# Adding the relative bias of windowed attention on VectorE instead of TensorE, and running the exponentials in place

## The chip, the cores and the metric

The kernel runs on one core of a Trainium2 chip. The metric is the device time of one execution in microseconds; three executions of the kernel before took 389.59, 389.60 and 390.54 us, median 389.6 us. The engines named below are those of the profile: PE (TensorE, matmuls; PEld is its weight load), DVE (VectorE), ACT (ScalarE), POOL (GpSimd) and SP (SyncE, which here only issues DMAs). Each engine works through its own instruction list in order, and the engines meet through semaphores.

## The reference

The input is `x`, 8 images of 64 channels and 32x32 pixels, float32. The first half is a window-attention block, the second a gated convolution block. What the change touches is the softmax of the attention:

```python
attn = jnp.einsum('bnhd,bmhd->bhnm', q * scale, k)          # 8x8 windows: N = 64 positions, 8 heads, d = 8
bias = rel_bias_table[REL_IDX.reshape(-1)].reshape(N, N, HEADS)
attn = attn + bias.transpose(2, 0, 1)[None]                  # the same bias for every window and image
attn = jax.nn.softmax(attn, axis=-1)
out = jnp.einsum('bhnm,bmhd->bnhd', attn, v).reshape(Bn, N, C)
return out @ w_proj + b_proj
```

Around it stand a layer norm before (over channels), the residual add, a second layer norm, an MLP with GELU, and then the second block: a pointwise convolution with ReLU, a gate that picks 32 of 64 channels per image, and three depthwise convolutions (3x3, 5x5, 7x7) fused with a pointwise one, computed on PE as one 7x7 convolution.

## The kernel before

Both halves of the batch lie side by side on the 128 partitions (two images of 64 channels), so 4 image pairs of 1024 pixels give 4096 columns, cut into `NG = 8` groups of `G = 512` columns. A group holds 8 windows of 64 pixels (times two images). The attention is a software pipeline written out by hand: each engine has a function `step(g, ...)`, and in the step of group g it also does the maxima pass of group g+1 (`nxt`), the first layer norm with keys and queries of group g+2 (`far`), and the projection, residual and second layer norm of group g-1 (`prev`). There are 8 steps. The order of the calls in `step` is the order on the engine; nothing else sets it.

What one step does for its own group g:

- PE, `scores(g, w)` for each window w = 0..7 writes a PSUM bank of 128x512 (128 rows = 64 keys of two images, 512 columns = 8 heads x 64 queries) by five passes of 512 columns: three of keys times queries in split precision (L793), one that adds the relative bias (L795, `reverse` times `rel`), one that subtracts each row's maximum (L796). Two banks, `PROB0` and `PROB0 + 1`, are used in turn: scores(g, w) waits until window w-2 has been read out.
- ACT, `exponentials(g, w)` (L558): exp from that bank to `probs` in SBUF, 128x512.
- PE, `weighted_values` (L809) and `sums` (L818) for windows 0 to 3 after the fourth exponential, and for windows 4 to 7 at the end of the step, both into the bank `PV`.
- DVE, `divide_by_sums(g, quad)`: a reciprocal (L1120) and a product (L1122), once for each half. The second half's one comes last in DVE's step and so runs beside the start of PE's next step.

The maxima pass of the next group: `scores_for_max(g+1, w)` on PE is two passes (L774, and L775 with the same `rel`, flipped), `take_maximum` on DVE is a reduction of one bank (L1106), with three banks in rotation; after the eighth, PE transposes the maxima (L779), DVE negates and spreads them (L1112 to L1115), and PE's next step begins with them.

Beside them on ACT, between the exponentials: four copies of the values (L553), two squares of the centred input (L512, L513), the evacuation of the projection (L562), the logarithm and exponential of the inverse deviation (L518, L520), the cast of the residual (L566), two more squares (L570, L571), and the evacuations of keys and queries with two casts (L528, L535, L543). On DVE: two casts and two subtractions that split the second layer norm's output (L1144 and L277), the residual add in two instructions (L1128), the products of the two layer norms (L1092, L1133), the low parts of keys and queries (L1096, L1101). On POOL: the low parts of the inputs of PE's mean and variance passes (L277 with `parts`).

After the last `scores`, POOL clears `images` with eight memsets (L438) for the second block.

## Time and profile before

| | |
|---|---|
| median of 3 runs | 389.6 us |
| the profiled execution: its time, its span | 388.71 us, 386.9 us |
| PE busy | 331.2 us (86% of the span) |
| DVE busy | 259.4 us (67%) |
| ACT busy | 182.3 us (47%) |
| POOL busy | 126.8 us (33%) |
| the attention steps, start of step 0 to end of step 7 | about 35.9 to 211.4 us |

The span is what the profiler covers; 1.8 us of the execution lie outside it. Busy time of an engine is the union of its instructions. A matmul of 512 columns lasts 0.39 us in its own record, but the next one starts 0.23 us after it; the chain of waits shows the 0.23. In the same way an instruction of DVE or ACT may start a little before the one ahead of it has ended.

### The profile page before, as it was taken

Reading aid. Unit: us, or ns where it says so; the run is one execution under the profiler, and the core shown is the slowest. Engines: PE = TensorE matmul, PEld = TensorE weight load, DVE = VectorE, ACT = ScalarE, POOL = GpSimd, SP = SyncE. Lnnn points to the kernel's source line nnn. Section 1 sums busy time; section 2 is a strip of 40 time slices with the busy share of each in tenths; the row PEclk is TensorE's granted clock in tenths of the full one; section 3 lists DMA queues with packets and bytes.
Section 4 is the critical chain, followed back from the end, with each engine's and each line's share of the span. In section 5 each row is a group of like instructions: output and inputs, shape, how many; then the busy total and the mean of one; then the engine's idle time right before and its main releaser. Section 6 shows DMA issues by size and latency. Waiting matters only on the chain.

```text
span 386.9 us, 6319 instructions
## 1 busy us (share of the span) xinstructions
PE 331.2 (86%) x2432; PEld 227.4 (59%) x2432; DVE 259.4 (67%) x342; ACT 182.3 (47%) x303; POOL 126.8 (33%) x80
## 2 busy tenths in 40 slices
PE   1767999999999999999999579991674997899994
PEld 1454667767677776767676234440353775677773
DVE  7566183684847758485774954479895992999921
ACT  5345538475674756666436579892330200111200
POOL 5451102212131221210206602229675418765000
PEclk9989999999999999999999969997595998999999
DMA  7522641122122122222110000930000857277731
GB/s 180 107 68 71 142 87 53 48 68 71 49 69 51 49 59 60 70 52 64 49 41 2 0 2 1 200 83 0 2 0 0 169 121 144 58 155 159 150 81 27
DMA packets 31147, 27.68 MB, mean 72 GB/s; under 512 B 21008, under 2 KB 27664, under 8 KB 31120
## 3 DMA queue, kind: packets, MB, share of 16 engines
q1 hardware_dynamic: 30544, 26.50, 30.2%
q10 hardware_dynamic: 576, 0.81, 0.9%
q8 instruction: 18, 0.29, 0.3%
q14 instruction: 9, 0.07, 0.1%
HBM read 3.82 MB, written 2.10 MB: 15 GB/s over the span
## 4 chain that ended last, share of the span: by engine, by line
PE 62%; DVE 23%; ACT 4%; issue 4%; POOL 4%; SPq 1%; DMA 0%; DVEq 0%; ACTq 0%; POOLq 0%
PE psum L1023 12%; PE psum L793 11%; PE psum L725 4%; PE psum L809 4%; PE psum L774 4%; PE psum L796 3%; PE psum L795 3%; PE psum L775 3%; PE psum L818 3%; DVE maxima L1106 3%; DVE whole_w L1315 3%; PE psum L938 2%; POOL conv_w L462 2%; PE psum L949 2%; PE psum L752 2%
## 5 line engine op out<-in xcount | busy, mean ns | idle before, releaser
L1023 PE MATMUL psum<-shifted,conv_w 128*128 128x512 f32 x336 | 91.4, 436 | 7.2 <-DVE conv_w L277 2.9
L1023 PEld LDWEIGHTS psum<-shifted,conv_w 128*128 128x128 f32 x336 | 67.4, 203 | 31.0 <-DVE conv_w L277 4.5
L558 ACT ACTIVATE probs<-psum 128x512 f32<-128x512 f32 x64 | 38.3, 599 | 50.2 <-PE psum L796 49.4
L793 PE MATMUL psum<-q_heads,k_blocks 128*128 128x512 f32 x192 | 59.1, 416 | 0.0
L1106 DVE TENSOR_REDUCE maxima<-psum 128x8 f32<-128x512 f32 x64 | 41.0, 684 | 23.8 <-PE psum L775 23.8
L277 POOL TENSOR_TENSOR parts<-x,parts 128x256 fp32r<-128x256 f32 (+1 forms) x21 | 18.8, 911 | 103.9 <-ACT parts L507 59.0
L793 PEld LDWEIGHTS psum<-q_heads,k_blocks 128*128 128x128 f32 x192 | 34.8, 188 | 13.6 <-issue 7.1
L681 ACT CAST conv_w<-whole_w 128x1792 fp32r<-128x1792 f32 x7 | 11.8, 1688 | 64.6 <-DVE whole_w L1319 64.6
L725 PE MATMUL psum<-parts,center_average 128*128 128x512 f32 x64 | 23.2, 446 | 17.7 <-DVE parts L277 16.5
L277 POOL TENSOR_TENSOR parts<-square_logvar,parts 128x512 fp32r<-128x512 f32 x14 | 18.1, 1290 | 53.5 <-ACT square_logvar L571 27.5
L455 POOL TENSOR_TENSOR whole_w<-small,weights 128x1792 f32<-128x1792 f32 x8 | 30.4, 3798 | 8.3 <-DVE conv_w L1329 4.7
L774 PE MATMUL psum<-k_heads,q_blocks 128*128 128x512 f32 x64 | 27.1, 423 | 4.8 <-DMA k_heads<-k_parts 3.4
L1120 DVE RECIPROCAL inv_sum<-psum 128x256 f32<-128x256 f32 x16 | 28.0, 1748 | 3.3 <-PE psum L818 3.2
L1315 DVE TENSOR_TENSOR whole_w<-whole_w,product 128x1280 f32<-128x1280 f32 x8 | 21.6, 2699 | 7.6 <-POOL whole_w L455 7.0
L775 PE MATMUL psum<-rel,reverse 128*128 128x512 f32 x64 | 25.9, 404 | 0.0
L725 PEld LDWEIGHTS psum<-parts,center_average 128*128 128x128 f32 x64 | 12.1, 207 | 23.2 <-DVE parts L277 9.8
L796 PE MATMUL psum<-minus_max,pick 128*128 128x512 f32 x64 | 25.2, 393 | 0.0
L795 PE MATMUL psum<-rel,reverse 128*128 128x512 f32 x64 | 25.1, 392 | 0.0
L446 POOL TENSOR_TENSOR images<-square_logvar,images 128x512 f32 (+1 forms) x8 | 12.5, 1568 | 31.6 <-ACT images L658 31.6
L1339 DVE SCALAR_TENSOR_TENSOR x<-psum,weights,x 64x512 f32<-64x512 f32 x16 | 12.0, 750 | 12.7 <-PE psum L1023 12.4
L938 PE MATMUL psum<-normed,mlp_w 128*128 128x512 f32 (+1 forms) x64 | 19.8, 452 | 0.0
L809 PEld LDWEIGHTS psum<-probs,v_blocks 128*32 128x32 f32 x1024 | 15.0, 110 | 8.0 <-issue 8.0
(138 smaller groups left out, 561.3 us busy)
## 6 DMA issues: line engine op xcount, KB each, us to landing
shifted<-images SPq DMA_DIRECT2D x32, 332.5 KB, 5.5
k_blocks<-k_parts SPq DMA_DIRECT2D x32, 128.0 KB, 2.8
q_heads<-q_parts SPq DMA_DIRECT2D x128, 32.0 KB, 2.0
k_heads<-k_parts SPq DMA_DIRECT2D x64, 32.0 KB, 1.9
out<-x SPq DMA_DIRECT2D x8, 256.0 KB, 3.0
x<-in_x SPq DMA_DIRECT2D x6, 256.0 KB, 5.8
x<-in_x SPq DMA_DIRECT2D x4, 128.0 KB, 4.3
weights<-in_weights ACTq DMA_DIRECT2D x1, 464.0 KB, 6.9
```

Of the source, the lines that this page charges most:

```text
L277: return engine.tensor_tensor(low, whole, high.bitcast(F32), ALU.subtract)
L558: act.activation(probs[:, w, :], psum[:, PROB0 + w % 2, :], ACT.Exp).then_inc(S["ac_probs"], 1)
L725: ins = pe.matmul(psum[:, bank, :], center_average[:, which, :], parts[:, part, :], start=part == 0, stop=part == 1)
L774: pe.matmul(max_bank(w), q_blocks[:, w, :], k_heads[:, :, w * T:(w + 1) * T], start=True, stop=False)
L775: pe.matmul(max_bank(w), reverse[:], rel[:, 0, :], start=False, stop=True).then_inc(S["pe_max"], 1)
L793: pe.matmul(bank, k_blocks[:, w // (NW // 2), k_part, w % (NW // 2), :], q_heads[:, q_part, :, w * T:(w + 1) * T], start=k_part + q_part = ...
L795: pe.matmul(bank, reverse[:], rel[:, 1, :], start=False, stop=False)
L796: pe.matmul(bank, pick[:, w, :], minus_max[:, :, :], start=False, stop=True).then_inc(S["pe_scores"], 1)
L809: pe.matmul(psum[32 * j:32 * j + 32, PV, p * T:(p + 1) * T], v_blocks[:, par, at:at + 32], probs[:, w, head * T:(head + 1) * T], start=hh ...
L1023: ins = pe.matmul(psum[:, CONV0 + bh, :], conv_w[bh][:, w_part, t, :], img[:, y:y + H - 1:2, x0:x0 + W], start=t == 0 and w_part + part == ...
L1106: dve.tensor_reduce(maxima[:, w * NH:(w + 1) * NH], max_bank(w).rearrange("p (h t) -> p h t", t=T), AX.X, ALU.max).then_inc(S["dv_max"], 1)
L1315: dve.tensor_tensor(window, window, product5[:], ALU.add).then_inc(S["dv_product"], 1)
```

## The change

The bias is added by DVE when it moves the scores out of PSUM, and the PE pass for it goes. For that the bias must lie in SBUF in the layout of the scores: PE makes it once, in the set-up, in the bank `PROB0`, and ACT copies it to the new tile `rel_by_key` (128x512). From then on DVE's `add_bias(g, w)` writes `probs` = scores + `rel_by_key`, and ACT's exponential reads and writes `probs` in place. PE's wait for a free bank is now a wait for DVE (`dv_biased`) where it was one for ACT (`ac_probs`). DVE's step gets eight more instructions, placed among the others by hand. The maxima pass keeps its own bias pass (L775).

```diff
             def exponentials(g, w):
-                act.wait_ge(S["pe_scores"], NW * g + w + 1)
-                act.activation(probs[:, w, :], psum[:, PROB0 + w % 2, :], ACT.Exp).then_inc(S["ac_probs"], 1)
+                act.wait_ge(S["dv_biased"], NW * g + w + 1)
+                act.activation(probs[:, w, :], probs[:, w, :], ACT.Exp).then_inc(S["ac_probs"], 1)
...
             act.wait_ge(S["weights_ready"], 1)
-            act.wait_ge(S["rel_ready"], 1)
+            act.wait_ge(S["pe_rel"], 1)
+            act.copy(rel_by_key[:], psum[:, PROB0, :]).then_inc(S["ac_rel_kept"], 1)
             step(0, 1, 2, 3, None, 0)
...
                 if not (isinstance(g, int) and NW * g + w < 2):
-                    pe.wait_ge(S["ac_probs"], NW * g + w - 1)
+                    pe.wait_ge(S["dv_biased"], NW * g + w - 1)
+                elif w == 0:
+                    pe.wait_ge(S["ac_rel_kept"], 1)
...
-                pe.matmul(bank, reverse[:], rel[:, 1, :], start=False, stop=False)
                 pe.matmul(bank, pick[:, w, :], minus_max[:, :, :], start=False, stop=True).then_inc(S["pe_scores"], 1)
...
             pe.wait_ge(S["rel_ready"], 1)
+            pe.matmul(psum[:, PROB0, :], reverse[:], rel[:, 1, :], start=True, stop=True).then_inc(S["pe_rel"], 1)
             centered(1)
...
+            def add_bias(g, w):
+                dve.wait_ge(S["pe_scores"], NW * g + w + 1)
+                if not (isinstance(g, int) and g == 0):
+                    dve.wait_ge(S["pe_pv"], 2 * g - 1 + w // (NW // 2))
+                dve.tensor_tensor(probs[:, w, :], psum[:, PROB0 + w % 2, :], rel_by_key[:], ALU.add).then_inc(S["dv_biased"], 1)
+
             def step(g, nxt, far, prev, older, par):
+                add_bias(g, 0)
                 if older is not None:
                     high_of_normed2(older)
+                add_bias(g, 1)
+                if older is not None:
                     for bh in range(2):
                         low_of_normed2(older, bh)
+                add_bias(g, 2)
                 if prev is not None:
                     add_residual(prev)
+                add_bias(g, 3)
+                add_bias(g, 4)
                 if far is not None:
                     normalise(far)
                 if nxt is not None:
-                    for w in range(3):
-                        take_maximum(nxt, w)
+                    take_maximum(nxt, 0)
+                    take_maximum(nxt, 1)
+                add_bias(g, 5)
+                if nxt is not None:
+                    take_maximum(nxt, 2)
                 divide_by_sums(g, 0)
                 if nxt is not None:
-                    for w in range(3, NW):
-                        take_maximum(nxt, w)
+                    take_maximum(nxt, 3)
+                add_bias(g, 6)
+                if nxt is not None:
+                    take_maximum(nxt, 4)
+                    take_maximum(nxt, 5)
+                add_bias(g, 7)
+                if nxt is not None:
+                    take_maximum(nxt, 6)
+                    take_maximum(nxt, 7)
                     spread_maxima(nxt)
```

The lines of code after the change stand a few numbers further down: what was L1106 is L1110, L1120 is L1124, and so on.

DVE, one step in the middle of the attention, before (`normed<-rstd` is the output of the second layer norm, `x<-square_logvar` the residual add):

```order
L1144 CAST normed<-rstd 64x512 [waits dv_whole2]
L1144 CAST normed<-rstd 64x512
L277 TENSOR_TENSOR normed<-rstd,normed 64x512 [waits dv_high2] x2
L1128 TENSOR_TENSOR x<-square_logvar,x 128x4x8x8 [waits ac_proj]
L1128 TENSOR_TENSOR x<-square_logvar,x 128x4x8x8
L1092 TENSOR_TENSOR normed<-psum,rstd 128x512 [waits ac_rstd]
L1106 TENSOR_REDUCE maxima<-psum 128x8 [waits pe_max] x3
L1120 RECIPROCAL inv_sum<-psum 128x256 [waits pe_pv]
L1122 TENSOR_TENSOR attended<-psum,inv_sum 128x256 [waits dv_inv]
L1106 TENSOR_REDUCE maxima<-psum 128x8 [waits pe_max] x5
```

The same place after, from the third bias addition of the step to the eighth:

```order
L1161 TENSOR_TENSOR probs<-psum,rel_by_key 128x512 [waits pe_pv,pe_scores]
L1132 TENSOR_TENSOR x<-square_logvar,x 128x4x8x8 [waits ac_proj]
L1132 TENSOR_TENSOR x<-square_logvar,x 128x4x8x8
L1161 TENSOR_TENSOR probs<-psum,rel_by_key 128x512 [waits pe_pv,pe_scores] x2
L1096 TENSOR_TENSOR normed<-psum,rstd 128x512 [waits ac_rstd]
L1110 TENSOR_REDUCE maxima<-psum 128x8 [waits pe_max] x2
L1161 TENSOR_TENSOR probs<-psum,rel_by_key 128x512 [waits pe_pv,pe_scores]
L1110 TENSOR_REDUCE maxima<-psum 128x8 [waits pe_max]
L1124 RECIPROCAL inv_sum<-psum 128x256 [waits pe_pv]
L1126 TENSOR_TENSOR attended<-psum,inv_sum 128x256 [waits dv_inv]
L1110 TENSOR_REDUCE maxima<-psum 128x8 [waits pe_max]
L1161 TENSOR_TENSOR probs<-psum,rel_by_key 128x512 [waits pe_pv,pe_scores]
```

The first two additions stand ahead of the two casts and between the casts and the subtractions; the sixth stands ahead of the reciprocal, the seventh and eighth among the last five maxima.

PE, from the queries of group 1 to the third window of step 0, before:

```order
L752 MATMUL psum<-normed,qkv_w 128x512
L793 MATMUL psum<-q_heads,k_blocks 128x512 [waits dv_minus,k_blocks_in0,weights_ready,q_heads_in0,weights_in,po_pick]
L793 MATMUL psum<-q_heads,k_blocks 128x512 x2
L795 MATMUL psum<-rel,reverse 128x512
L796 MATMUL psum<-minus_max,pick 128x512
L757 MATMUL psum<-qkv_w,normed 128x128 x4
```

and after:

```order
L754 MATMUL psum<-normed,qkv_w 128x512
L797 MATMUL psum<-q_heads,k_blocks 128x512 [waits ac_rel_kept,dv_minus,k_blocks_in0,weights_ready,q_heads_in0,weights_in,po_pick]
L797 MATMUL psum<-q_heads,k_blocks 128x512 x2
L799 MATMUL psum<-minus_max,pick 128x512
L759 MATMUL psum<-qkv_w,normed 128x128 x4
```

The bias pass is gone, and the first scores wait for `ac_rel_kept`.

ACT at the same place, before:

```order
L528 ACTIVATE k_parts<-psum,qkv_bias 128x2x256 [waits pe_k]
L535 ACTIVATE q_parts<-psum,q_bias 128x2x256 [waits pe_q]
L543 CAST q_blocks<-q_parts 64x8x64 [waits pe_max,ac_q_high]
L543 CAST q_blocks<-q_parts 64x8x64
L558 ACTIVATE probs<-psum 128x512 [waits pe_scores,rel_ready,weights_ready]
```

and after:

```order
L529 ACTIVATE k_parts<-psum,qkv_bias 128x2x256 [waits pe_k]
L536 ACTIVATE q_parts<-psum,q_bias 128x2x256 [waits pe_q]
L544 CAST q_blocks<-q_parts 64x8x64 [waits pe_max,ac_q_high]
L544 CAST q_blocks<-q_parts 64x8x64
L629 COPY rel_by_key<-psum 128x512 [waits pe_rel,weights_ready]
L559 ACTIVATE probs<-probs 128x512 [waits dv_biased]
```

The copy that sets `ac_rel_kept` stands behind the evacuation of the queries of group 1 and its two casts.

## Rows read from the trace of the kernel before

**Rows 1.** The page, part 1: busy time of each engine.

```profile
PE 331.2 (86%) x2432; PEld 227.4 (59%) x2432; DVE 259.4 (67%) x342; ACT 182.3 (47%) x303; POOL 126.8 (33%) x80
```

**Rows 2.** Windows: one step each; window, length, busy (instructions) by engine, granted clock.

```profile
105.12:128.30 23.18, 23.12 (x241) 16.52 (x241) 15.88 (x26) 15.11 (x29) 5.28 (x5) 1.00 0.22 58
174.70:195.80 21.10, 20.18 (x233) 15.18 (x233) 14.01 (x23) 9.85 (x19) 2.59 (x2) 1.00 0.24 61
195.80:206.00 10.20, 10.20 (x114) 7.56 (x115) 6.54 (x9) 4.32 (x8) 1.29 (x1) 1.00 0.07 19
```

**Rows 3.** Chain of waits, pieces of one step: start, us, what.

```profile
106.01 0.23 PE psum L795
...
115.76 0.43 PE psum L774
...
116.88 0.69 PE psum L793 x3
...
123.58 1.30 DVE maxima L1106 x2
...
124.92 0.43 PE psum L779 x2
125.36 1.05 PE psum L752 x2
126.41 1.03 PE psum L809 x64
127.44 0.86 PE psum L818 x16
```

**Rows 4.** Timeline, DVE, the same step: start, us, line, operation, idle before.

```profile
105.22 1.75 DVE L1120 RECIPROCAL inv_sum<-psum 128x256 f32<-128x256 f32 x1
...
107.34 0.85 DVE L1144 CAST normed<-rstd 64x512 fp32r<-64x512 f32 x2
108.22 1.40 DVE L277 TENSOR_TENSOR normed<-rstd,normed 64x512 fp32r<-64x512 f32 x2
111.75 0.78 DVE L1128 TENSOR_TENSOR x<-square_logvar,x 128x256 f32<-128x256 f32 x2 [2.13 <-ACT square_logvar L562]
114.12 0.69 DVE L1092 TENSOR_TENSOR normed<-psum,rstd 128x512 f32<-128x512 f32 x1 [1.59 <-ACT rstd L520]
...
121.24 1.88 DVE L1106 TENSOR_REDUCE maxima<-psum 128x8 f32<-128x512 f32 x3
```

**Rows 5.** Timeline, ACT, the same step.

```profile
107.40 1.55 ACT L553 COPY v_blocks<-psum 64x256 f32<-64x256 f32 x4 [0.29 <-PE psum L757]
...
109.47 0.59 ACT L512 ACTIVATE parts<-psum 128x512 fp32r<-128x512 f32 x1
...
110.42 0.62 ACT L558 ACTIVATE probs<-psum 128x512 f32<-128x512 f32 x1
111.03 0.69 ACT L562 ACTIVATE square_logvar<-psum,proj_bias 128x512 f32<-128x512 f32 x1
...
113.46 0.63 ACT L520 ACTIVATE rstd<-square_logvar 128x512 f32<-128x512 f32 x1
114.00 0.58 ACT L558 ACTIVATE probs<-psum 128x512 f32<-128x512 f32 x1
```

**Rows 6.** Chain of waits, into step 0.

```profile
35.04 0.87 PE psum L752 x2
...
37.29 0.62 ACT q_blocks L543
...
41.64 1.28 POOL parts L277
```

**Rows 7.** Windows, columns as in rows 2: PE idles from 21.7 us, then works.

```profile
25.00:26.50 1.50, 1.38 (x3) 1.16 (x4) 0.15 (x1) 0.00 (x0) 0.52 (x1) 0.50 0.69 157
```

**Rows 8.** Timeline, the end of step 7.

```profile
208.75 10.02 POOL L438 MEMSET images<- 128x1444 f32 x8
...
213.75 5.88 DVE L1144 CAST normed<-rstd 64x512 fp32r<-64x512 f32 x2
```

More of the change, by code:

```diff
@@ L177, in conv_seq_kernel @@
         parts = at("parts", [128, 2, G], F32R)
+        rel_by_key = at("rel_by_key", [128, NH * T])
         normed2 = at("normed2", [128, 2, COLS], F32R)
@@ L229, in conv_seq_kernel @@
             "x_high", "ac_x1", "po_pick", "x_low", "square_low", "x1_low", "square2_low", "dv_whole2", "dv_high2",
-            "pe_xc", "pe_var", "pe_q", "pe_k", "pe_v", "pe_max", "pe_maxt", "pe_scores", "pe_pv", "pe_proj", "pe_xc2", "pe_var2",
+            "pe_xc", "pe_var", "pe_q", "pe_k", "pe_v", "pe_max", "pe_rel", "ac_rel_kept", "dv_biased", "pe_maxt", "pe_scores", "pe_pv", "pe_proj", "pe_xc2", "pe_var2",
             "ac_sq", "ac_log", "ac_rstd", "ac_q_high", "ac_k_high", "ac_v", "ac_probs", "ac_proj", "ac_sq2", "ac_log2", "ac_rstd2",
@@ L1190, in _ @@
             q_low(1, 1)
+            dve.wait_ge(S["ac_rel_kept"], 1)
             step(0, 1, 2, None, None, 0)
```

## The prediction, made before the changed kernel ran

> **What bounds the kernel now.** I read the busy times first: PE 86% of the span, DVE 67%, ACT 47% [rows 1]. Then one attention step by itself, in the windows: of 23.18 us PE is busy for 23.12, DVE for 15.88, ACT for 15.11 [rows 2]. So inside the steps PE is the bound. The chain of waits confirms it: it runs on PE piece after piece and leaves it once a step, for 1.30 us of DVE maxima, after which PE transposes them [rows 3]. The profile marks five such steps (1 to 5) of 23.2 us; step 6, without keys and queries of a later group, takes 21.10 us [rows 2]; step 7 is shorter still; before them step 0 takes 22.8 us (35.9 to 58.7).
>
> **What PE gains.** A pass of 512 columns moves the chain by 0.23 us [rows 3], not by the 0.39 us of its record. Eight go in each step: 8 x 0.23 = 1.84 us, a step of 21.3 us if nothing else were late; over eight steps 14.7 us. Each addition that replaces them is a DVE instruction on a PSUM bank and an SBUF tile, 128x512. The trace has this very form in the layer norm's product: 0.69 us [rows 4]. Behind each other such instructions start 0.60 us apart (three maxima of 0.69 us end after 1.88 us [rows 4]: (1.88 - 0.69) / 2). I take 0.60 us of DVE's time and 0.72 us until the result is seen (0.69 and 0.03 for the semaphore); the other end is 0.69 of its time each, if the two semaphores it waits for keep it from overlapping. DVE's work in a step becomes 15.88 + 8 x 0.60 = 20.7 us, against 21.3 for PE. That is 97%: DVE can only keep up if it never waits, and in this order it must wait, since the additions, the residual and the maxima each wait for another engine.
>
> **The new loop.** So I walked one step with the order of each engine and these durations, from the moment when DVE starts the reciprocal of the former group's second half (0.19 us into PE's step). At each piece I took the later of its engine and its input. The same walk of the order before gives 23.16 us a step, against 23.18 in the trace, with the PE passes in full and the other engines' starts within 0.1 us. The path that decides after the change:
> - DVE: 0.19 to start, reciprocal and product 2.12 (105.22 to 107.34 [rows 4]), first addition 0.72: 3.03. Before, the first exponential could start when its scores were there (1.5 us into the step), beside that reciprocal; now it stands behind it.
> - ACT, in order: exp 0.53, four copies 1.53, exp 0.53, two squares 0.96 (109.47 to 110.42 [rows 5]), exp 0.53, evacuation of the projection 0.69 + 0.04: 4.81, to 7.84. An exp from PSUM holds ACT for about 0.48 to 0.50; one from SBUF, as L520 is, lasts 0.63 and holds it for 0.54 (113.46 to 114.00 [rows 5]). I take 0.53 for the new ones.
> - DVE: residual 0.77 (two in 0.78 [rows 4]), fourth addition 0.72: to 9.33. ACT: fourth exp 0.67: to 10.00.
> - PE: weighted values 1.03, sums 0.86 [rows 3], two windows of maxima 1.12 (115.76 to 116.88 [rows 3]), scores of window 5 in four passes 0.92, and 0.20 until DVE sees them: to 14.13. Before, PE began the weighted values at 8.7 us.
> - DVE without a gap: addition 5, a maximum, 1.20; the reciprocal pair of this group's first half, 2.12; then five maxima and two additions, 7 x 0.60 = 4.20, and 0.12: to 21.77.
> - PE: transpose 0.40, queries 1.05, weighted values 1.03, sums 0.86 [rows 3]: 25.11.
> A second path, squares to POOL's low part to the variance pass, ends 0.5 us earlier, so it takes over at once if the first is shortened. The step is 25.11 us against 23.18, +1.93 us, although PE has 1.84 us less to do: some 3.8 us of waits appear on PE (about 1.9 before the variance, 0.5 before the weighted values, the rest before the last maxima and their transpose). The five steps give +9.6 us.
>
> **Scores wait for a copy, once.** In the set-up PE's new pass lies before an idle stretch (it waits from 21.7 to 25.1 us for keys) and costs nothing; if that cover were gone, one pass at the low clock, about 0.43. But the copy to `rel_by_key` stands behind ACT's casts of group 1, which end at 37.91 us (37.29 + 0.62 [rows 6]); it takes 0.69 like other PSUM to SBUF moves, and PE's first scores wait for it: 38.63. PE was free at 35.91 (35.04 + 0.87 [rows 6]): +2.72 us. Queued behind this wait is all of step 0, and the first addition behind that. From there step 0 by the same walk: first scores and addition 1.84, on ACT exp, copies, exp, squares 3.71, POOL's low part 1.29 and 0.05 (1.28 [rows 6]), variance 0.46, scores 0.92, weighted values and sums 1.89, maxima 1.12, scores 1.12, then the DVE stretch 7.64 and the PE end 3.34: 23.38 against 22.84, +0.54 us.
>
> **Steps 6 and 7.** In step 6 the squares are gone and the third addition decides, behind DVE's casts and subtractions: 0.19 + 2.12 + 0.60 + 0.80 + 0.60 + 1.38 + 0.72 = 6.41 (casts and subtractions from [rows 4]); exp and projection 1.26, residual and addition 1.49, exp 0.67: 9.83; PE 4.13, DVE 7.64, PE without queries 2.29: 23.89 against 21.10 [rows 2], +2.79. Step 7 has no maxima pass, so PE has nothing to do beside these waits: 9.83, then weighted values, sums, scores and 0.20 make 12.84, addition, exp and squares 2.37, POOL's low part 1.29: POOL starts its memsets 16.50 us into the step. Before it was 208.75 - 195.80 = 12.95 [rows 2, 8]: +3.55. The end hangs on those memsets: DVE's cast, ready at 213.75, lasts until they are over, 5.88 us for two where a step elsewhere shows 0.85 [rows 4, 8]. That cover would hide up to 5 us of a delay of DVE alone, but here the memsets are delayed as much (the product before the casts ends about 4.8 us before them), so nothing is hidden. From there the tail moves as a whole; the second block is not touched.
>
> **The sum.** 2.72 + 0.54 + 9.6 + 2.79 + 3.55 = 19.2 us. The profiled execution took 388.7, so 407.9; the median of the runs is 0.9 above it: 389.6 + 19.2 = 408.8, rounded to 409.
>
> **A rule against the exponentials in place.** The trace has exponentials of 0.63 us from SBUF (L520) and 0.60 from PSUM [rows 5]; the four on the path cost 0.1 to 0.2 us a step more in place, which the sum holds. The Trainium skill, in "VectorE: DVE Perf Modes", section "The TRN2 errata", gives ScalarE a fixed cost of 224 cycles from SBUF and 172 from PSUM; at its 1.2 GHz an estimate by that page is 0.04 us for each. By it the sum would be the same within 0.3 us.
>
> **Rivals.**
> - *PE stays the bound.* DVE finds the additions' inputs ready and its 20.7 us fit into 21.3. Then 389.6 - 14.7, and 2.7 back for the copy: about 378. For it: the busy shares, DVE at 67% [rows 1]. Against it: the exponentials of windows 0 to 2 lose their head start of 1.5 us, and ACT had only 0.5 us of idle time between copies and projection. 6%. The Trainium skill ("Perfetto Trace Analysis", "Identifying the Most-Contended Engine") has the engine with the highest occupancy optimised first; read alone, that rule would give this rival.
> - *A draw.* The chain is 2 us shorter than my walk, since a wait in it overlaps: 8 steps at 23.1. 389 to 391. 3%.
> - *The additions do not overlap.* At 0.69 each, five on the path: +0.45 a step, +3.6 to +4.5 in all: 413. It is the same mechanism, dearer. 20%.
> - *The clock falls.* PE idles 2.7 us before the first scores. After the idle stretch from 21.7 to 25.1 the granted clock was 0.50 (1.2 GHz) for 2.8 us [rows 7], with passes of 0.43 instead of 0.23; the same again would cost up to 1.4 us, of which ACT's path hides part: 410. The stalls inside a step, 1.9 us at most, are shorter than that. 15%, within the likeliest.
> - *DVE escapes the memsets.* If its product comes after their end, the blocked cast shrinks from 5.9 to 0.8, up to 4.7 us back: 404. It needs DVE 4.8 us later than POOL's start allows. 5%, within the likeliest.
>
> **Chances and range.** My loop, 71%, clock (15) and memsets (5) in it; with dearer additions 20%; PE-bound 6%, draw 3%. The measurement of this kernel tells about 0.3% (1.2 us) from no change. Faster 6%, within it 3%, slower 91%. The bounds of addition (0.55 to 0.69) and exp (0.48 to 0.54) give 404.5 to 414; with the clock and the tail 402 to 416. The two cases below leave 9% outside.
>
> **What would show it.** Right: steps of about 25 us; in the chain, DVE and ACT between PE's pieces; PE waiting before the variance pass (L727) for POOL and before the transpose (L781) for DVE; DVE busy for about 20.7 us of a step; first scores at 38.6 us; additions of 0.69 us. Wrong: steps of 21 to 22 us with PE busy throughout (first rival), additions or exponentials longer than their rows, or the stretch of maxima no longer without gaps.

## The result and the profile after

The kernel after takes 420.1 us (median; 418.4 to 421.3) against 389.6 before: a ratio of 1.077, 95% interval 1.073 to 1.082. It is slower, as forecast, but by 30.5 us where the forecast was 19.2. Its profiled execution took 420.31 us, with a span of 418.5 us. Medians and ranges here leave out executions more than 1.5% above the fastest of the same kernel, which was one, of e1.

From the page of the kernel after, busy times (part 1), the chain by engine (part 4) and two groups of part 5, to lay beside [rows 1]:

```profile
PE 337.1 (81%) x2369; PEld 224.0 (54%) x2369; DVE 297.7 (71%) x406; ACT 183.7 (44%) x304; POOL 126.6 (30%) x80
...
DVE 38%; PE 37%; ACT 7%; issue 7%; POOL 5%; DMA 2%; SPq 2%; DVEq 0%; ACTq 0%; POOLq 0%
...
L559 ACT ACTIVATE probs<-probs 128x512 f32<-128x512 f32 x64 | 40.3, 630 | 92.2 <-DVE probs L1161 92.1
...
L1161 DVE TENSOR_TENSOR probs<-psum,rel_by_key 128x512 f32<-128x512 f32 x64 | 43.7, 686 | 20.4 <-PE psum L799 19.1
```

PE has 63 instructions fewer and is busy 5.9 us longer: that is the first sign that its clock has changed. It is not all clock: in a step at full clock PE is busy for 22.1 us, not 21.3, as a pass ahead of a stall counts with its whole record. An addition lasts 686 ns and an exponential in place 630, both as estimated. The chain, which lay on PE for 62% before and on DVE for 23%, is now on DVE for 38% and on PE for 37%.

The windows of the kernel after, columns as in [rows 2]: four steps, three single microseconds inside the third, and step 7 up to POOL's memsets.

```profile
64.50:89.70 25.20, 22.08 (x236) 14.89 (x232) 18.61 (x29) 15.05 (x29) 5.25 (x5) 1.00 0.21 55
...
98.00:99.00 1.00, 1.00 (x3) 0.86 (x4) 1.00 (x3) 0.00 (x0) 0.00 (x0) 0.65 0.77 178
99.00:100.00 1.00, 1.00 (x4) 0.66 (x3) 0.10 (x1) 0.86 (x2) 0.00 (x0) 0.50 0.21 63
100.00:101.00 1.00, 1.00 (x22) 0.50 (x24) 0.39 (x1) 0.97 (x2) 0.00 (x0) 0.50 0.12 36
...
116.10:142.60 26.50, 23.55 (x237) 15.88 (x233) 20.91 (x34) 15.07 (x29) 5.23 (x5) 0.94 0.20 51
142.60:168.00 25.40, 22.11 (x236) 14.77 (x232) 20.93 (x34) 14.98 (x29) 5.26 (x5) 1.00 0.20 53
...
221.50:239.80 18.30, 13.24 (x120) 8.84 (x116) 11.78 (x18) 5.93 (x11) 2.44 (x2) 0.91 0.01 3
```

Where the clock stays at 1.00, a step lasts 25.2 to 25.5 us, with PE idle for 3.1 to 3.3 of them; the walk gave 25.11. Where it falls, the step lasts 26.4 to 26.5: PE works at 0.50 for about 3.4 us (125.6 to 129 in one step, 98.3 to 101.7 in another), and some 1.2 us are lost. Steps 2, 3, 5 and 7 hold one such stretch and step 6 two; in step 0 one begins 0.9 us behind the first scores.

The chain of waits in step 4, at full clock (start, us, what), against [rows 3]:

```profile
142.81 1.68 DVE inv_sum L1124
...
145.14 0.70 DVE probs L1161
145.87 0.63 ACT probs L559
...
148.61 0.60 ACT parts L513
149.20 0.50 ACT square_logvar L514
149.77 1.27 POOL parts L278
151.09 0.73 PE psum L727 x2
...
153.01 1.10 PE psum L812 x64
154.11 0.86 PE psum L821 x16
...
157.06 0.69 DVE probs L1161
157.76 0.60 DVE maxima L1110
158.35 1.68 DVE inv_sum L1124
160.39 0.68 DVE maxima L1110
...
163.47 1.21 DVE maxima L1110 x2
164.72 0.45 PE psum L781 x2
165.67 0.69 DVE minus_max L1119
166.36 0.60 DVE rstd L1137
166.96 0.66 DVE k_parts L1100
167.62 0.66 DVE q_parts L1105
168.28 1.68 DVE inv_sum L1124
```

It goes DVE, ACT, POOL, PE, DVE, PE: waits of the kind that the walk had, but on two stretches not the path that it called deciding. In the first third the path through the squares and POOL (L513, L514, L278) decides, which the walk had 0.5 us behind; and the chain leaves the step on DVE's own work after the maxima, where the walk left it on PE.

The timeline of the kernel after (start, us, engine, line, operation, idle before) shows what stands ahead of the low clock, and the end of step 7, against [rows 8]:

```profile
97.94 0.93 PE L727 MATMUL psum<-parts,center_average 128*128 128x512 f32 x2 [2.07 <-POOL parts L278]
98.67 1.48 PE L797 MATMUL psum<-q_heads,k_blocks 128*128 128x512 f32 x3
...
151.09 0.73 PE L727 MATMUL psum<-parts,center_average 128*128 128x512 f32 x2 [2.23 <-POOL parts L278]
...
239.84 10.03 POOL L439 MEMSET images<- 128x1444 f32 x8
...
244.14 1.76 DVE L1124 RECIPROCAL inv_sum<-psum 128x256 f32<-128x256 f32 x1 [1.27 <-PE psum L821]
...
246.28 4.45 DVE L1148 CAST normed<-rstd 64x512 fp32r<-64x512 f32 x2
```

PE waits 2.07 us for POOL, and the three passes of scores behind it take 1.48 us, where those of the first scores take 0.93 (below). In step 4 it waits 2.23 us and keeps its clock: the same stall lowers it in some steps and not in others. At the end the casts last until the memsets are over, as in [rows 8].

The chain of the kernel after, into step 0, against [rows 6]:

```profile
35.59 0.87 PE psum L754 x2
...
37.84 0.61 ACT q_blocks L544
...
38.48 0.59 ACT rel_by_key L629
39.07 0.35 issue
39.42 0.93 PE psum L797 x3
```

The first scores wait 2.96 us (36.46 to 39.42) for the copy, and the clock falls right behind: it is 0.66 on average from 39 to 44 us. They start 3.86 us later than before: 2.96 are the wait, 0.35 the overlap with the pass ahead that is lost with it (before, they started at 35.56, ahead of the record's end at 35.91), and 0.55 a later end of the set-up. This last is not the change's: e10, whose set-up is that of the kernel before, starts its first scores at 36.43 us, 0.87 later.

Both kernels need 168 to 169 us from the end of the memsets on (218.77 to 386.9 before, 249.87 to 418.5 after). So nearly all that was lost, 31.1 of 31.6 us in the profiled executions, was lost ahead of that. By the records' starts:

| stretch | before, us | change forecast | change after | e9: early copy, no low clock |
|---|---|---|---|---|
| to the first scores | 35.56 | +2.7 | +3.9 | +0.4 |
| step 0 | 23.12 | +0.5 | +2.0 | +1.3 |
| steps 1 to 5 | 115.94 | +9.6 | +13.9 | +10.4 |
| step 6 | 21.11 | +2.8 | +6.0 | +3.0 |
| step 7, to the memsets | 13.02 | +3.5 | +5.3 | +3.7 |
| sum | 208.75 | +19.2 | +31.1 | +18.8 |

The last column is an experiment below; it is what the sum of the forecast, less the copy, is to be compared with.

### The profile page after: what moved, and what is told of

The parts are those of the page before. It is cut to its first block, busy times and chain, and to the rows that moved or that the text cites. A ratio compares the mean times of both kernels' runs of the same rounds, so it can differ in the third digit from the quotient of the medians.

```text
span 418.5 us, 6315 instructions
## 1 busy us (share of the span) xinstructions
PE 337.1 (81%) x2369; PEld 224.0 (54%) x2369; DVE 297.7 (71%) x406; ACT 183.7 (44%) x304; POOL 126.6 (30%) x80
## 4 chain that ended last, share of the span: by engine, by line
DVE 38%; PE 37%; ACT 7%; issue 7%; POOL 5%; DMA 2%; SPq 2%; DVEq 0%; ACTq 0%; POOLq 0%
PE psum L1027 11%; DVE maxima L1110 7%; DVE inv_sum L1124 6%; DVE probs L1161 5%; PE psum L797 4%; PE psum L812 4%; PE psum L821 3%; DVE whole_w L1342 2%; PE psum L942 2%; POOL conv_w L463 2%; POOL parts L278 2%; PE psum L727 2%; DMA probs<-in_rel_table 2%; PE psum L953 2%; ACT probs L559 2%
## 5 line engine op out<-in xcount | busy, mean ns | idle before, releaser
L1027 PE MATMUL psum<-shifted,conv_w 128*128 128x512 f32 x336 | 92.5, 440 | 6.6 <-DVE conv_w L278 2.9
L559 ACT ACTIVATE probs<-probs 128x512 f32<-128x512 f32 x64 | 40.3, 630 | 92.2 <-DVE probs L1161 92.1
L797 PE MATMUL psum<-q_heads,k_blocks 128*128 128x512 f32 x192 | 61.3, 429 | 5.2 <-ACT rel_by_key L629 3.0
L1161 DVE TENSOR_TENSOR probs<-psum,rel_by_key 128x512 f32<-128x512 f32 x64 | 43.7, 686 | 20.4 <-PE psum L799 19.1
L278 POOL TENSOR_TENSOR parts<-x,parts 128x256 fp32r<-128x256 f32 (+1 forms) x21 | 19.1, 922 | 121.0 <-ACT parts L508 62.0
L1110 DVE TENSOR_REDUCE maxima<-psum 128x8 f32<-128x512 f32 x64 | 41.7, 683 | 15.8 <-PE psum L777 15.8
L727 PE MATMUL psum<-parts,center_average 128*128 128x512 f32 x64 | 23.6, 453 | 26.5 <-POOL parts L278 13.6
L278 POOL TENSOR_TENSOR parts<-square_logvar,parts 128x512 fp32r<-128x512 f32 x14 | 17.9, 1275 | 66.3 <-ACT square_logvar L514 37.7
L776 PE MATMUL psum<-k_heads,q_blocks 128*128 128x512 f32 x64 | 28.2, 440 | 6.9 <-DMA k_heads<-k_parts 3.7
L1124 DVE RECIPROCAL inv_sum<-psum 128x256 f32<-128x256 f32 x16 | 28.0, 1750 | 3.3 <-PE psum L821 3.3
L727 PEld LDWEIGHTS psum<-parts,center_average 128*128 128x128 f32 x64 | 11.7, 205 | 33.6 <-POOL parts L278 17.8
L812 PEld LDWEIGHTS psum<-probs,v_blocks 128*32 128x32 f32 x1024 | 19.7, 133 | 14.5 <-issue 14.5
L812 PE MATMUL psum<-probs,v_blocks 128*32 128x64 f32 x1024 | 22.5, 255 | 5.4 <-issue 5.3
L777 PE MATMUL psum<-rel,reverse 128*128 128x512 f32 x64 | 26.2, 410 | 0.0
L776 PEld LDWEIGHTS psum<-k_heads,q_blocks 128*128 128x128 f32 x64 | 12.8, 200 | 16.5 <-issue 7.2
```

The costliest lines, as they stand in the source:

```text
L278: return engine.tensor_tensor(low, whole, high.bitcast(F32), ALU.subtract)
L559: act.activation(probs[:, w, :], probs[:, w, :], ACT.Exp).then_inc(S["ac_probs"], 1)
L727: ins = pe.matmul(psum[:, bank, :], center_average[:, which, :], parts[:, part, :], start=part == 0, stop=part == 1)
L776: pe.matmul(max_bank(w), q_blocks[:, w, :], k_heads[:, :, w * T:(w + 1) * T], start=True, stop=False)
L797: pe.matmul(bank, k_blocks[:, w // (NW // 2), k_part, w % (NW // 2), :], q_heads[:, q_part, :, w * T:(w + 1) * T], start=k_part + q_part = ...
L812: pe.matmul(psum[32 * j:32 * j + 32, PV, p * T:(p + 1) * T], v_blocks[:, par, at:at + 32], probs[:, w, head * T:(head + 1) * T], start=hh ...
```

## The experiments

In the expectations, A is the account above: the walked path of waits, with the clock lowered by PE's own stalls and the copy on the path. Its rival was that DVE's added load by itself, or a dearer instruction, sets the steps; each expectation states the one that its run tests. Lines shown are edits of the kernel after unless it says otherwise.

**e1: fill PE's stalls.** Eight spare passes of 512 columns, into a bank that nobody reads, stand where PE would wait: ahead of the variance pass in steps 0 to 5, ahead of the weighted values in 6 and 7. They add no work to any other engine.

```diff
+            def spare_passes(count):
+                for _ in range(count):
+                    pe.matmul(psum[:, MISC0, :], reverse[:], rel[:, 0, :], start=True, stop=True)
+
-            def variance(n):
+            def variance(n, spare=0):
+                if spare:
+                    pe.wait_ge(S["dv_q_low"], n)
+                    spare_passes(spare)
                 pe.wait_ge(S["square_low"], n + 1)
...
-                    variance(far)
+                    variance(far, 8)
                 scores(g, 4)
+                if far is None:
+                    pe.wait_ge(S["dv_q_low"], NG)
+                    pe.wait_ge(S["ac_log2"], g - 1)
+                    spare_passes(8)
```

> The changed kernel, with eight spare passes of 512 columns on PE (into the bank MISC0, overwritten right after) in the stall ahead of the variance pass of steps 0 to 5, and ahead of the first weighted values of steps 6 and 7, so that PE has 1.84 us to do in a stall of 2.0 to 2.3 us. Theory A (my walk of the loop was right, and what it left out is the clock, which in the changed kernel fell to 0.50 for 3 to 5 us in steps 2, 3, 5, 6 and 7): the granted clock stays at 1.00 from step 1 on, every one of steps 1 to 5 takes 25.5 us like the one that kept its clock, step 6 about 24.3; the time is 412 to 414 us. Theory B (the low clock costs nothing, since DVE's chain sets the step; steps of 26.4 us come from DVE or ACT): the time stays at 420 us within 1 us, with the clock at 1.00.

Measured: 413.1 us (409.5 to 414.0), ratio 1.056 (1.050 to 1.062). PE does more and the kernel is 7.0 us faster. From 46 to 216 us the granted clock is 1.00, and steps 1 to 6 last 25.24, 25.20, 25.20, 25.50, 25.19 and 25.27 us. The forecast for step 6, 24.3, missed: its last 2.5 us lie in a low stretch that begins at 216.3 us, behind a stall of 1.66 us ahead of the transpose, where no spare pass stands. The profiled execution, 415.8, is above its three others: part of its set-up lay at the low clock and its first scores came at 42.1 us, so only its steps are read.

**e2: copy early.** The copy to `rel_by_key` goes behind ACT's squares of group 1, where ACT is idle.

```diff
             square_of_centered(1)
+            act.wait_ge(S["pe_rel"], 1)
+            act.copy(rel_by_key[:], psum[:, PROB0, :]).then_inc(S["ac_rel_kept"], 1)
             inverse_deviation(1)
```

> The changed kernel, with the copy of the bias to SBUF moved on ACT from behind the evacuations of group 1 to behind the squares of group 1, where ACT is idle. Theory A (the copy held PE's first scores back by 3.0 us and the idle stretch then lowered the clock for 3.5 us): the first scores start where PE is free, at about 36.4 us, without a low clock at 40 to 44 us; the time falls by 3.5 to 4.5 us, to about 416. Theory B (step 0 is bound by the additions and ACT's chain in any case): it falls by 2.4 us or less, to 417.5 to 420.

Measured: 414.8 us (413.4 to 416.3), 1.064 (1.059 to 1.068): 5.3 us back. The first scores start at 35.61 us instead of 39.42. The low stretches inside the steps are still there (five of steps 0 to 6 last 25.9 to 26.7, two 25.16), and step 0, which A had free of them, has one as well, behind a stall of 2.37 us:

```profile
43.30:46.70 3.40, 3.27 (x22) 2.24 (x26) 0.31 (x1) 1.32 (x2) 0.07 (x1) 0.50 0.85 223
```

Whether the copy cost more than its wait isn't shown. In the profiled executions the first scores come 3.8 us earlier (the wait of 2.96, the overlap of 0.35, 0.5 of set-up), the time from there to the memsets is the same within 0.2 us (200.4 and 200.6), and 2.5 us are won behind the start of the memsets, where the copy has no part.

**e3 and e4: the load without the waits.** e3 has no relative bias in the softmax: no PE pass for it in the scores, no addition, exponentials from PSUM as before. e4 is e3 with eight DVE additions a step at the places of the change, which nobody waits for (`rel` + `rel` to an unused tile).

```diff
-                dve.wait_ge(S["pe_scores"], NW * g + w + 1)
...
-                dve.tensor_tensor(probs[:, w, :], psum[:, PROB0 + w % 2, :], rel_by_key[:], ALU.add).then_inc(S["dv_biased"], 1)
+                dve.tensor_tensor(unused[:], rel[:, 1, :].bitcast(F32), rel[:, 0, :].bitcast(F32), ALU.add).then_inc(S["dv_unused"], 1)
```

> The kernel before, without PE's bias pass for the final scores (L795) and with nothing in its place: the relative bias is left out of the softmax, everything else is as before. It gives the most that taking the pass off PE can bring. Theory A (walk of the step: after the pass is gone the maxima's chain through DVE and the transpose is nearly as long as PE's work): steps of 21.9 us, 379.7 us. Theory B (PE is the only bound): 64 passes of 0.23 us less, steps of 21.35 us, 374.9 us.

> As the kernel without the bias pass, but DVE does one addition of 128x512 (two constant tiles from SBUF into a tile that nobody reads) at each of the 64 places where the changed kernel has its additions. Nobody waits for them, and they wait for nothing but the one before; the exponentials read PSUM as before. The bias is left out of the softmax. It has the changed kernel's load on DVE without its waits. Theory A (walk: the load costs 8.5 of the 30 us, the waits the rest): steps of 23.0 us, 388 us. Theory B (DVE's load is what slows the kernel): within 5 us of 420. Theory C (load is hidden): 380 us as without it.

Measured: e3 382.1 us (381.0 to 383.8), 0.980 (0.976 to 0.984), steps of 22.10. Removing all 64 passes with nothing in their place gives 8.0 us (390.2 beside it), not 14.7: PE was the bound by so little that another path, through ACT and POOL, is late next (PE waits 0.50 us for POOL ahead of each variance pass of steps 1 to 5). e4 392.6 us (389.6 to 394.2), 1.006 (1.003 to 1.008), steps of 23.57. The page's group, one step of e4, and its timeline of DVE and POOL in the step ahead of that:

```profile
L1156 DVE TENSOR_TENSOR unused<-rel 128x512 f32<-128x512 f32 x64 | 49.2, 769 | 0.9
...
106.60:130.20 23.60, 22.05 (x237) 14.83 (x233) 21.63 (x34) 14.89 (x29) 5.66 (x5) 1.00 0.22 56
...
88.94 1.66 DVE L1156 TENSOR_TENSOR unused<-rel 128x512 f32<-128x512 f32 x1
...
88.36 1.69 POOL L278 TENSOR_TENSOR parts<-square_logvar,parts 128x512 fp32r<-128x512 f32 x1 [2.94 <-ACT square_logvar L514]
```

DVE is busy for 21.63 us of the step, more than in the kernel after (20.9). The 769 ns are a mean of two kinds: 58 of the 64 additions last 0.68 to 0.69 us, and six, one of them in each of steps 2 to 5, 1.2 to 1.66 us, beside POOL. POOL's subtraction beside them lasts 1.68 to 1.69 us in these steps and 1.29 in e3, and PE's stall behind it is 0.9 us against 0.5. So e4 is no clean copy of the load: some 0.4 us a step are of its own making, part of what it lies above A (23.57 for 23.0, 392.6 for 388). B is refuted all the same. The load is worth at most 10.5 us over e3, and the kernel after 38.0: the other 27.5 us are waits, the copy's among them, and what they do to the clock.

**e5 and e6: part of the windows.** The additions of windows 5 to 7 only, and of 0 to 4 only; the others keep PE's pass and the exponential from PSUM.

```diff
+        BY_VECTOR = (5, 6, 7)        # e6: (0, 1, 2, 3, 4)
...
             def exponentials(g, w):
+                if w in BY_VECTOR:
                     act.wait_ge(S["dv_biased"], biased(g, w))
                     act.activation(probs[:, w, :], probs[:, w, :], ACT.Exp).then_inc(S["ac_probs"], 1)
+                else:
+                    act.wait_ge(S["pe_scores"], NW * g + w + 1)
+                    act.activation(probs[:, w, :], psum[:, PROB0 + w % 2, :], ACT.Exp).then_inc(S["ac_probs"], 1)
...
+                if w not in BY_VECTOR:
+                    pe.matmul(bank, reverse[:], rel[:, 1, :], start=False, stop=False)
```

> Only windows 5, 6 and 7 of each group get their bias from DVE, at the changed kernel's places; windows 0 to 4 keep PE's pass and an exponential straight from PSUM. The copy stays where the change has it. Theory A (walk): without the additions 0 to 4 the exponentials start early again; what stays is the stretch of maxima, reciprocal and three additions ahead of the transpose: steps of 23.7 us at full clock, 397 us, and up to 3 us more where the clock falls. Theory B (it is the number of additions that counts, 30 us for 8): 3 of 8 give 401 us. Theory C (the late additions do all the harm): 410 or more.

> The other part: only windows 0 to 4 get their bias from DVE, windows 5 to 7 keep PE's pass. Theory A (walk): the chain reciprocal, first addition, ACT's row of exponentials, residual, fourth addition, fourth exponential, weighted values is as long as in the changed kernel; three additions fewer in the late stretch, but three PE passes more: steps of 24.5 us at full clock, 404 us, and with the clock falling in most steps, as in the changed kernel, 407 to 411. Theory B (by the number of additions, 5 of 8): 409 without any difference between this place and the other; the two parts together give the whole loss. Theory C (the early ones are harmless): 392 or less.

Measured: e5 400.5 us (396.5 to 401.3), 1.023 (1.019 to 1.028), steps of 23.74, for 23.7 by the walk. e6 409.3 us (409.2 to 411.4), 1.049 (1.046 to 1.053): steps of 24.61 to 24.65 at full clock (walk 24.5) and 25.95 in the two with a low stretch. By the steps the walk holds for other sets of windows too. By the times alone B, which counts additions, is met as well: 401 and 409 forecast, 400.5 and 409.3 measured, and the two losses, 10.2 and 19.1 us, come to 29.3, near the whole. What speaks against it is that, less the 5.3 us of the copy that both contain, e5 costs 4.9 us for three windows and e6 13.8 for five, so the first ones are the dearer (0.55 and 1.42 us a step at full clock); e7 and e8 settle it.

**e7: the same load in another order.** All eight additions stay on DVE, the copy is early, and DVE's list is changed: the reciprocal of the former half stands behind the first addition, the next two additions ahead of the casts, the fifth behind the layer norm's product, the reciprocal of this half ahead of all maxima.

```diff
                 add_bias(g, 0)
+                if prev is not None:
+                    divide_by_sums(prev, 1)
+                add_bias(g, 1)
+                add_bias(g, 2)
                 if older is not None:
                     high_of_normed2(older)
-                add_bias(g, 1)
+                add_bias(g, 3)
...
                     normalise(far)
+                add_bias(g, 4)
+                divide_by_sums(g, 0)
...
-                divide_by_sums(g, 1)
```

> All eight additions on DVE as in the changed kernel, with the early copy, but in another order of DVE's step: addition 0 ahead of the former group's second reciprocal and product, additions 1 and 2 right behind these, then the casts, addition 3, the subtractions, the residual, the first layer norm's product, addition 4, the reciprocal of the first half ahead of the first maximum, addition 5, maxima 0 to 2, wait: maxima 1 to 3, addition 6, maxima 4 and 5, addition 7, maxima 6 and 7. Same instructions, same load. Theory A (it is the order, that is, who waits for whom, not the load): steps of 23.5 us at full clock, 394 us, up to 5 more with the clock. Theory B (DVE's load of 20.9 us a step is what binds, or waits that no order avoids): it stays within 4 us of the run with the early copy alone, 411 to 417.

Measured: 396.4 us (395.5 to 397.0), 1.017 (1.013 to 1.020), which is 18.4 us less than e2, with the same instructions. Windows of e7, one step, columns as in [rows 2], and PE's variance pass in that step:

```profile
106.80:130.80 24.00, 21.84 (x237) 14.87 (x233) 21.48 (x34) 15.23 (x29) 5.27 (x5) 1.00 0.22 56
```

```profile
114.62 0.73 PE L727 MATMUL psum<-parts,center_average 128*128 128x512 f32 x2 [1.65 <-POOL parts L278]
```

DVE is busy for 21.5 of 24.0 us, and no step has a low stretch: PE's stall ahead of the variance pass is 1.6 us in steps 1 to 5, not 2.0 to 2.2. That the load sets the time is refuted; what is left over [rows 2] is 0.8 us a step. Some of the 18.4 us are the clock's: over e9, which keeps its clock in the steps too, e7 gains 12.

**e8: put it where nobody waits.** Only windows 2, 4 and 6 go to DVE, in an order found with the walk; copy early.

```diff
+        BY_VECTOR = (2, 4, 6)
...
             def step(g, nxt, far, prev, older, par):
-                add_bias(g, 0)
                 if older is not None:
                     high_of_normed2(older)
-                add_bias(g, 1)
+                add_bias(g, 2)
...
                     normalise(far)
+                add_bias(g, 4)
                 if nxt is not None:
                     take_maximum(nxt, 0)
+                divide_by_sums(g, 0)
...
                     take_maximum(nxt, 2)
-                divide_by_sums(g, 0)
+                add_bias(g, 6)
```

> Only windows 2, 4 and 6 get their bias from DVE, each in a place where DVE was idle before and nobody waits for it at once: addition 2 between the casts and the subtractions, 4 behind the first layer norm's product, 6 behind maximum 2, and the reciprocal of the first half behind maximum 0. The copy is early. Theory A (walk): steps of 22.6 us against 23.2, 4 us less than the kernel before: 385.6 us. Theory B (every addition costs more through the waits than the 0.23 us of PE it saves): 390 to 395. Theory C (clock: small stalls lower it although PE is busy for 97% of a step): about 390.

Measured: 387.2 us (385.0 to 388.5), 0.992 (0.989 to 0.995), with steps of 22.77 against 23.19; POOL's memsets start at 206.25 us instead of 208.75. That is 3.1 us, of 4 forecast. Its window: PE is busy for 22.68 of 22.80 us. The reciprocal was moved too, but that alone can't give it: in [rows 2] PE stood idle for only 0.06 us of the step, so what PE no longer does, three passes, is what counts.

```profile
104.60:127.40 22.80, 22.68 (x241) 15.90 (x237) 18.78 (x29) 15.39 (x29) 5.29 (x5) 1.00 0.23 59
```

**e9: e1 and e2 together.**

> The changed kernel with both mendings together: spare PE passes in the stalls (as in the run with them alone) and the early copy of the bias. Theory A (the loss of 30 us is my walked chain of waits, 17 us without the copy, plus the copy, plus the clock, and nothing else): steps of 25.2 us, clock at 1.00 from the first scores to the end of step 6, 406 to 408 us. Theory B (something else of the change costs too): 410 or more, with steps over 25.4.

Measured: 408.8 us (408.2 to 410.8), 1.049 (1.045 to 1.053). Windows of e9, one step and steps 0 to 6 together, and its PE timeline at the variance pass:

```profile
111.00:136.20 25.20, 23.92 (x241) 16.40 (x242) 20.93 (x35) 15.07 (x29) 5.27 (x5) 1.00 0.21 53
...
36.00:214.00 178.00, 165.17 (x1676) 113.60 (x1676) 141.25 (x221) 98.71 (x183) 30.26 (x28) 1.00 0.24 60
```

```profile
117.79 1.08 PE L741 MATMUL psum<-rel,reverse 128*128 128x512 f32 x4
119.07 0.73 PE L727 MATMUL psum<-parts,center_average 128*128 128x512 f32 x2 [0.21 <-POOL parts L278]
```

With passes at L741 where PE stood idle, the stall before L727 is 0.21 us here (0.45 at most in steps 1 to 5) instead of 2.0 to 2.2, and the clock is 1.00 in all steps. Against e2, which differs in the spare passes alone, that is 6.0 us. In its last column the table above has what the walked path costs by itself: 18.8 us, 0.4 of it set-up, where the forecast without the copy was 16.5.

**e10: the memsets later, in the kernel before.** POOL starts its memsets only when DVE has made the casts of group 6, so that the two no longer meet.

```diff
             pool.wait_ge(S["pe_scores"], NW * NG)
+            pool.wait_ge(S["dv_high2"], NG - 1)
             for b4 in range(NB4):
```

> The kernel before; only POOL's memsets of the images (10 us) now wait until DVE has done the two casts that come behind step 7. Theory A (those casts lasted 5.9 us instead of 0.85 because POOL's memsets held them up, and the tail hangs on them): the casts take 0.85 us, the time falls by 4.0 to 4.7 us to 385.5. Theory B (the casts wait for something else, or the memsets, now later, hold up another instruction of DVE or the ReLU that needs the cleared images): it stays within 1.5 us.

Measured: 384.1 us (383.5 to 386.6), 0.987 (0.983 to 0.990). The timeline of e10, against [rows 8], one window of the kernel before and the same of e10, and PE's variance pass of the last group, before and in e10:

```profile
214.72 0.85 DVE L1145 CAST normed<-rstd 64x512 fp32r<-64x512 f32 x2
...
215.69 10.02 POOL L439 MEMSET images<- 128x1444 f32 x8 [5.91 <-DVE normed L1145]
```

```profile
222.00:230.00 8.00, 4.80 (x12) 3.35 (x12) 2.89 (x5) 5.74 (x8) 0.00 (x0) 0.57 0.01 2
```

```profile
222.00:230.00 8.00, 7.50 (x30) 4.25 (x32) 4.22 (x7) 7.69 (x12) 4.13 (x4) 1.00 0.01 2
```

```profile
223.30 1.22 PE L725 MATMUL psum<-parts,center_average 128*128 128x512 f32 x2 [5.16 <-DVE parts L277]
```

```profile
219.87 0.73 PE L726 MATMUL psum<-parts,center_average 128*128 128x512 f32 x2 [0.77 <-DVE parts L277]
```

The casts take 0.85 us instead of 5.88, PE's stall ahead of the next variance pass is 0.77 us instead of 5.16, and the clock from 222 to 230 us, 0.57 in the kernel before, stays at 1.00. A wait of 5.9 us put on POOL makes the kernel 5.8 us faster. That is over A's 4.0 to 4.7, which had no gain of the clock in it.

**e11: e8 and e10 together.**

> The kernel with windows 2, 4 and 6 on DVE, and the later memsets. Theory A (the two gains lie in different stretches and add up): 387.2 - 4.4 = 382.8 us. Theory B (they overlap, since the steps' gain ended at the memsets): 385 or more.

Measured: 380.1 us (379.6 to 382.2), 0.976 (0.973 to 0.979), steps of 22.77. It beats the kernel before by 9.8 us (389.9 beside it), 0.9 more than the two gains together (3.1 and 5.8), which is within the spread of the executions, and is the fastest of all.

## Why the prediction was wrong

- *PE's gain, 0.23 us a pass.* Right as a bound, but never to be had: e3 shows 8.0 us for all of it, and the prediction's 21.3 us a step for this case was itself too low by 0.8 (22.10).
- *The loop.* Right in its length and its kind. 25.11 walked, 25.2 to 25.5 measured at full clock; both waits on PE (POOL before L727, DVE before L781) and DVE's 20.7 us a step (20.9) came as written. The deciding path did not in its first third: it was the second one, over squares and POOL, called 0.5 us shorter. That the step came out nearly as long is due to the two being so close. What is over, 0.1 to 0.4 us a step, was not followed up. e5, e6 and e7 bear out the walk: 23.74, 24.6 and 23.94 against 23.7, 24.5 and 23.5, the last 0.4 off.
- *The copy.* The wait was right, 2.96 us for 2.72. The sum took it from the end of the pass ahead and so missed the lost overlap, 0.35.
- *Steps 6 and 7, the memsets.* With a full clock +3.0 and +3.7 (e9) for +2.79 and +3.55; the cast was held up until the memsets ended, as forecast, and the tail moved as a whole.
- *The step that failed* is the rival on the clock: "The stalls inside a step, 1.9 us at most, are shorter than that. 15%, within the likeliest", with a price of "up to 1.4 us" once. The one idle stretch of [rows 7], 3.4 us, was taken as the shortest that matters, though no row showed that a shorter one is harmless. In the run the stall before the variance pass was 2.0 to 2.2 us, and behind it the clock fell to 0.50 in three of steps 1 to 5, 1.2 us each; it fell twice in step 6 (about 3 us; once behind a stall of only 1.66 us) and once in step 7 (1.6). With 0.65 us in step 0 that is 8.8 us from the first scores to the memsets, by which the kernel after is longer there than e9, where the stalls are filled. Of the 11.9 us by which the sum fell short (31.1 for 19.2), 8.8 are this term, 1.1 lie ahead of the first scores (0.55 of them set-up, no effect of the change), and 1.9 are what the walk was short of.
- *The rivals.* PE as the bound and the draw are out. Additions were not dearer (686 ns). DVE did not escape the memsets (4.45 us for the casts). The range's upper end, 416, was made of those bounds and of one fall of the clock; seven were seen after 39 us.
- *Occupancy.* The Trainium skill ("Perfetto Trace Analysis", "Identifying the Most-Contended Engine") has the engine with the highest occupancy optimised first. The prediction left out that the same section of the Trainium skill sets TensorE apart: the busy share of its matmuls is no good measure, and headroom there goes by the share of weight loads and by the rate of useful arithmetic. The runs agree with that exception: PE's matmuls were at 86%, its weight loads at 59% and DVE at 67% [rows 1], and taking 64 passes from PE for nothing gave 2%, giving them to DVE cost 8%. Nor was occupancy the whole of it: delaying POOL, at 33% the least busy of the four, gave 1.3%.

Open: why the same stall lowers the clock in steps 2, 3 and 5 and not in 1 and 4. Which steps are hit differs between runs (e2 has steps 2 and 5 free), which fits the spread of 3 us between the executions of the kernel after. That filling the stalls keeps the clock up is shown by e1 and e9; what decides between the steps isn't. Nor was a spare pass put ahead of the first scores alone, so what the copy cost beyond its wait and the lost overlap stays open.

## What to carry to other kernels

Before work is moved off a full engine, walk one period with every engine's order and see who waits for whom behind the new instruction; the same eight additions cost 18 us more in one order than in another, and three of them at places where nobody waits gained 3.1. Then count each stall that the walk puts on TensorE, price its wait and the microseconds at half clock that may follow, and widen the range by both for every period, even where the stalls are shorter than the one behind which the trace of before shows the clock low. A transfer of work is to be tried on the window that has slack, not on all of them.

## What the runs showed of the hardware

- Stalls of TensorE of 2.0 to 2.2 us, ahead of the variance pass, once a step, were followed by 3.4 us at a granted clock of 0.50 (its 1.2 GHz level) in three of steps 1 to 5 of the kernel after, in three of e2 and in two of e6. Stalls of 1.6 us at the same place were not, in any of these five steps of e7. In step 0 a stall of 2.4 us was, in e2, and was not in e7. A stall of 1.66 us ahead of the transpose of step 6 was, in the kernel after and in e1, and was not in e2 and e9. So no length that is safe follows from these runs. Passes whose result nobody reads kept the clock at 1.00 for 178 us (e9).
- DVE's cast from SBUF to SBUF stands still while POOL's eight memsets run (5.88 us before, 4.45 after, 0.85 in e10). The reciprocal, which reads PSUM, isn't held up beside them (1.76 us at 244.14, 1.75 in [rows 4]).
- A DVE addition of two SBUF tiles, 128x512, lasted 0.68 to 0.69 us in 58 of 64 places of e4, as with one operand in PSUM (686 ns), and 1.65 to 1.66 us in the five places where it ran beside POOL's subtraction for 1.1 us; in four of them POOL's subtraction was longer too, 1.68 to 1.69 us for 1.29 in e3.
